# Fused attention and routed FFN on one core: value products issued for two neighbouring key tiles at a time, between the scores of pairs of tiles

## The reference

```python
qkv = layernorm(x) @ Wqkv                 # q: 32 x 16, k: 16, v: 16
scores = einsum('bqhd,bkd->bhqk', q, k) * 16 ** -0.5
scores = where(pos_k <= pos_q, scores + slopes * (pos_k - pos_q), -1e30)
attn = einsum('bhqk,bkd->bqhd', softmax(scores), v).reshape(B, S, H)
x = x + attn @ Wo
y = layernorm(x)
result = y @ W_base.T + b_base
route_w = top-2 of softmax(y @ W_gate.T), renormalised
x = x + result + einsum('bner,eor->bno', (y @ A) * route_w, B)
```

## Time and profile before

| | |
|---|---|
| median of 3 runs | 790.23 us (788.66 to 791.53) |
| profiled execution, first to last instruction | 788.3 us (its own time with what lies around the span is not given apart) |
| TensorE matmul / VectorE / ScalarE / GpSimd busy | 691.0 / 576.1 / 356.9 / 187.6 us |
| granted TensorE clock, mean | 0.956; 1.00 from 170 to 660 us |
| chain that ended last | TensorE 67%, DMA 14%, VectorE 11% |

### The profile page before, as it was taken

The page is one execution under the profiler, slowest core; times in us unless marked ns, Lnnn a source line. Parts: engine busy times, 40 slices in busy tenths (PEclk is TensorE's granted clock), DMA queues, the critical chain, the costliest instruction groups (busy, mean ns, idle before and its releaser), DMA issues.

```text
span 788.3 us, 16078 instructions
## 1 busy us (share of the span) xinstructions
PE 691.0 (88%) x4224; PEld 299.5 (38%) x4224; DVE 576.1 (73%) x1851; ACT 356.9 (45%) x493; POOL 187.6 (24%) x340
## 2 busy tenths in 40 slices
PE   4486535989999999999999999999999996699997
PEld 2243212333344344344334334334433453355553
DVE  6175344989988988989898998898892372366664
ACT  2133010246676666676666666666666410011111
POOL 0010101132242242133233224224233311222221
PEclk9888677999999999999999999999999999699999
DMA  9559799111043052062061085500000189400001
GB/s 235 71 150 128 113 129 224 67 37 64 31 59 55 29 70 43 27 74 52 16 96 39 16 108 91 84 30 16 15 29 30 37 141 162 117 27 27 27 27 53
DMA packets 37592, 56.06 MB, mean 71 GB/s; under 512 B 6028, under 2 KB 19468, under 8 KB 37524
## 3 DMA queue, kind: packets, MB, share of 16 engines
q1 hardware_dynamic: 35468, 49.17, 35.1%
q0 software_dynamic: 1792, 6.29, 2.4%
q10 hardware_dynamic: 288, 0.07, 0.0%
HBM read 35.72 MB, written 19.79 MB: 70 GB/s over the span
## 4 chain that ended last, share of the span: by engine, by line
PE 67%; DMA 14%; DVE 11%; issue 4%; SPq 3%; ACT 1%; DVEq 0%; POOL 0%; POOLq 0%; ACTq 0%
PE psum L606 19%; PE psum L561 16%; PE psum L588 9%; PE psum L630 5%; PE psum L652 5%; DMA q_dram<-work 4%; PE psum L585 4%; DMA arena<-q_dram 4%; DMA x_sb<-in_x 4%; DVE psum L967 3%; PE psum L522 3%; DMA out<-wqkv_sb 3%; DVE negm L972 2%; PE psum L647 1%; PE psum L662 1%
## 5 line engine op out<-in xcount | busy, mean ns | idle before, releaser
L791 ACT ACTIVATE work<-psum 128x1024 f32<-128x1024 f32 (+1 forms) x320 | 289.7, 943 | 161.6 <-PE psum L588 136.2
L967 DVE CUSTOM_DVE_ANT_0 psum<-psum,future 128x384 f32<-128x384 f32 (+3 forms) x512 | 240.0, 517 | 33.1 <-PE psum L561 26.2
L561 PE MATMUL psum<-k_op,arena 106*128 106x512 bf16 (+3 forms) x768 | 209.5, 331 | 35.6 <-DMA arena<-q_dram 20.2
L972 DVE TENSOR_REDUCE negm<-psum 128x1 f32<-128x512 f32 x256 | 163.1, 684 | 29.1 <-PE psum L561 28.4
L606 PE MATMUL psum<-work,v_op 128*32 128x512 f32 (+3 forms) x1536 | 164.3, 500 | 0.4 <-POOL work L1152 0.4
L588 PE MATMUL psum<-arena,k_op 109*128 (+4 forms) x640 | 158.6, 316 | 1.0 <-ACT work L791 0.8
L1152 POOL TENSOR_SCALAR_AFFINE_SELECT work<-work 128x512 f32<-128x512 f32 x128 | 81.6, 637 | 276.5 <-ACT work L791 276.5
L561 PEld LDWEIGHTS psum<-k_op,arena 106*128 (+1 forms) x768 | 69.9, 97 | 192.7 <-issue 95.7
L522 PE MATMUL psum<-work,wqkv_sb 128*128 128x512 f32 (+1 forms) x160 | 83.1, 642 | 15.9 <-issue 15.2
L585 PE MATMUL psum<-arena,k_op 116*128 (+1 forms) x512 | 85.1, 221 | 0.0
L588 PEld LDWEIGHTS psum<-arena,k_op 109*128 109x128 bf16 x640 | 60.3, 98 | 35.7 <-ACT work L791 8.9
(11 more groups left out here) (84 smaller groups left out, 453.1 us busy)
## 6 DMA issues: line engine op xcount, KB each, us to landing
o_dram<-o_sb SPq DMA_DIRECT2D x32, 256.0 KB
q_dram<-work POOLq DMA_DIRECT2D x16, 384.0 KB, 3.1
arena<-q_dram SPq DMA_DIRECT2D x12, 512.0 KB, 17.8
arena<-q_dram SPq DMA_DIRECT2D x48, 128.0 KB, 5.9
arena<-o_dram SPq DMA_DIRECT2D x32, 128.0 KB, 8.9
arena<-rcp_dram SPq DMA_DIRECT2D x32, 128.0 KB, 9.4
out<-wqkv_sb SPq DMA_DIRECT2D x16, 256.0 KB, 2.0
x_sb<-in_x SPq DMA_DIRECT2D x3, 1024.0 KB, 9.0
```

What stands on the lines that cost most here:

```text
L561: last = nc.tensor.matmul(bank[:, a * width:(a + 1) * width], q_op[0:ROW_MAX, bass.ds(col, P)], k_op[0:ROW_MAX, b, k0:k0 + width], start=T ...
L791: nc.scalar.activation(probs[:, n % 4, heads * hp:heads * (hp + 1), 0:w], src, ACT.Exp).then_inc(exp_done, 1)
L967: last = nc.vector.tensor_tensor_reduce(keys, keys, future[:, CH - width:CH], -1.0, 3e38, ALU.add, ALU.min, negm[:, late, 0, j * QT + t:j ...
L972: nc.vector.tensor_reduce(dst, psum[:, idx % NSB, 0:len(js) * width].rearrange("p (a k) -> p a k", a=len(js)), AX_X, ALU.max, negate=True) ...
```

## The change

Only `pe_order` changes. The scores of a tile (both halves) are put in the list without values between them. After every odd tile the values of two tiles are put, those of tile n - 3 and of tile n - 2. The slots are spread over the new list by the same rule.

```diff
     for n, (late, t, off) in enumerate(TILES):
         w = CH - off
         if 1 <= k <= NK:
-            work.append((UH // HALVES[n] * w, ("scores", k - 1, (n, 0))))
-        m, v = (k - 1, n - LAG) if n >= LAG else (k - 2, n - LAG + NTI)
-        if 0 <= m < NK:
-            work.append((UH * (CH - TILES[v][2]), ("values", m, v)))
-        if 1 <= k <= NK and HALVES[n] == 2:
-            work.append((UH // 2 * w, ("scores", k - 1, (n, 1))))
+            work += [(UH // HALVES[n] * w, ("scores", k - 1, (n, hp))) for hp in range(HALVES[n])]
+        if n % 2:
+            for v in (n - 1 - LAG, n - LAG):
+                m, v = (k - 1, v) if v >= 0 else (k - 2, v + NTI)
+                if 0 <= m < NK:
+                    work.append((UH * (CH - TILES[v][2]), ("values", m, v)))
         if k == NK + 1 and n == LAG - 1:
             break
```

## The result

The changed kernel takes 834.45 us (median of 4 runs, 833.15 to 837.35), the kernel before 789.85 on the same chip: a ratio of 1.057, 95% interval 1.055 to 1.060. The profiled execution spans 835.2 us against 788.3.

The account below looks back on a forecast made before the run. TensorE's order was taken to set the time. A net 2.66 us a step gave 37.2 us for 14 steps, plus 2.2 and 1.6 for steps 1 and 16: 41.0 on 790.23, so 831.2 us, range 812 to 845.

Parts of the forecast that it names:

- What bounds the kernel: Steps 2 to 15: TensorE's order sets the time, busy 392.8 of 403.1 us; VectorE has a tenth to spare, ScalarE a third.
- Savings at the ends of runs: Runs of values groups on TensorE: 12 become 10 a step, at 0.21 us each, saving 0.42 us a step.
- Waits in the bursts: Scores in four halves wait for ScalarE to free two PSUM pairs: 0.65 + 0.86 + 0.86 + 0.66 + 1.07 = 4.10 us a step.
- The two copies: Output-bank copies in ScalarE's queue, between halves of tiles 1 and 5: waits of 0.66 us at tile 3, 0.77 at tile 6.
- VectorE's waits of 0.87 go: Tail of the step: TensorE's 0.87 us of waits for VectorE vanish, as VectorE clears its backlog after tile 7's later scores.
- rival 2: Slots before values: VectorE's waits stay or grow, 845 us; chance 0.07.
- The sum: Steps 2 to 15: 4.10 - 0.15 - 0.87 - 0.42 = 2.66 us a step, 37.2 us for 14 steps.
- Steps 1 and 16: First and last attention steps: 2.2 us more in step 1 and 1.6 us more in step 16.
- The signs: Profile after: steps of 31 to 32 us, TensorE's share near 0.90, gap before the copy, tile 6's second half 0.8 us late.
- only the ends count (783): All attention steps: 35 runs of values fewer at 0.21 us give 7.4 us faster, 783 us; chance 0.04.
- Hidden copies (815): ScalarE's two output-bank copies cost nothing, no wait at tile 3, giving 815 us; chance 0.08.
- No difference (790): Whole kernel: new waits only take the place of TensorE's present ones, no difference that counts; chance 0.02.

## Why the prediction was right

The forecast was 831.2 us, the result 834.45. Point by point:

- **What bounds the kernel.** Right: the time follows TensorE's order and its waits, and ScalarE's third of idle time covered nothing.
- **Savings at the ends of runs.** Taken at 0.21 us a run; the trace of the changed kernel gives 0.24. The groups of tiles 10 and 11 take 0.79 together (358.60 to 359.39) against 0.57 + 0.36 apart, 0.14 less, and the way in is 0.10 as before. So 0.48 a step and not 0.42.
- **Waits in the bursts, 4.10 us a step.** Measured 3.99 in the step shown. The large tiles agree within 0.01 at tiles 5 and 7. Tile 1 waits 0.24 less than worked out, since the start of this step runs a little slower than the pace (the slots of 128 and 256 columns from 355.37 take 0.56 us to the next scores where the pace gives 0.33), and a wait absorbs that.
- **The two copies.** Right in place and kind; 0.76 + 0.90 measured for 0.66 + 0.77, and 1.25 us a step came back when they were moved.
- **VectorE's waits of 0.87 go.** This term was mis-sized, and the reading under it was incomplete: 0.87 are not "the only large waits" of the kernel before. Later in the same step three slots of 384, 384 and 512 columns hold TensorE for 0.94 us, where the pace and the way into the values give 0.66, so 0.28 more for VectorE:

```profile
329.02 1.01 PE L561 MATMUL psum<-k_op,arena 106*128 106x384 bf16 x3
329.96 1.07 PE L606 MATMUL psum<-work,v_op 128*32 128x512 f32 x8
```

  Of 1.15 us, then, 0.59 stay in the step of the changed kernel: 0.41 at 373.16 to 373.79, some 0.12 at 362.92 to 363.58, and 0.06 at 375.11 to 375.88. 0.56 go, not 0.87, in the direction of rival 2. The microsecond that TensorE loses on tiles 6 and 7 clears VectorE's backlog in part alone; why not all of it was not tried by itself.
- **The sum.** In the step shown 3.99 - 0.15 - 0.56 - 0.48 = 2.80; it takes 31.59 us where the same step of the kernel before takes 28.54, so 3.05 more. The 0.25 between them are small losses that the walk has no term for, 0.18 of them at the slower start (0.23 over the pace, against 0.05 at 338.06 to 338.54). With the same paces taken off every distance from turn to turn in all 14 steps, waits before scores grow by 4.10 (from 0.18 to 4.28) where the prediction had 4.10 - 0.15, those between slots shrink by 0.58 (1.30 to 0.72) where it had 0.87, and the rest, the ends of runs above all, by 0.50 where it had 0.42. That makes the 3.02 of the two stretches; 2.66 was forecast.
- **Steps 1 and 16.** 0.7 for 2.2 and 2.7 for 1.6. Neither is a clean comparison. In step 1 the kernel before ran at the lower clock for a while (0.66 from 165 to 170 us) and the changed one did not (1.00), which flatters the change; what that is worth, where TensorE also waits for VectorE, I have not worked out. In step 16 it is the changed kernel that had the lower clock; that cost about 1.4 us (below), more than the 1.1 by which the step exceeds the forecast.
- **The signs.** The step of 31.72 us, TensorE's busy share of 0.91 (404.21 of 444.05), the gaps before both copies and the late second half of tile 6 came as said. The sign for rival 2, that waits for L967 and L972 still make over 1 us a step, was badly chosen: the view of waits gives 3.7 us a step, but nearly all of it is on weight loads, and it gave 4.0 before. The starts give 0.72.
- **The rivals.** That only the ends count (783) is refuted, most plainly by the run with all six pairs in one piece, at 873. The Trainium skill has, in "TensorEngine Tiling (Array Packing)", Overview, Key Properties, that changing the tiling mode drains TensorE. The 0.24 us of the rows agree with it, without showing that a drain is what takes them; it is a small term here. Hidden copies (815) did not happen: both had a gap of 1.24 us. No difference (790) fell with the first row of waits.

## What to carry to other kernels

An engine at two thirds of its time can still set the pace if its work arrives in bursts longer than the buffers in between: count how many producers' pieces stand side by side, and compare the time to the one that reuses a buffer (here 1.22 us) with the latency of a round through it (1.72). When one engine's order changes, look at every instruction of the others that stands between two events of it (the copy, here): its right place moves along, and that was two fifths of the loss here. Filler work belongs where the main engine would wait anyway.

## What was unexpected of the hardware

In step 16 of the changed kernel the granted clock of TensorE falls in the stretch with the long waits. Stretches of 5 us, columns as in the earlier trace rows:

```profile
650.00:655.00 5.00, 2.85 (x25) 0.80 (x24) 0.00 (x0) 4.40 (x6) 0.00 (x0) 1.00 0.01 3
655.00:660.00 5.00, 4.06 (x18) 0.90 (x22) 1.18 (x5) 3.96 (x6) 0.00 (x0) 0.73 0.13 51
660.00:665.00 5.00, 5.00 (x32) 2.25 (x24) 0.00 (x0) 2.66 (x4) 0.59 (x1) 0.93 0.01 2
```

TensorE was busy 2.85 of 5 us while ScalarE was busy 4.40; then the clock was at the lower of its two levels (1.2 GHz) for a part of the next stretches, and a pair of values groups took 3.30 us there where it takes 1.92 elsewhere:

```profile
657.91 3.30 PE L606 MATMUL psum<-work,v_op 128*32 128x512 f32 x16
...
665.06 1.92 PE L606 MATMUL psum<-work,v_op 128*32 128x512 f32 x16
```

So waits for another engine cost a second time here, about 1.4 us on that pair. It is not the change's work alone, and not every thin stretch does it. The run without slots between the values has such a dip in step 16 too, and two in the steps before, behind waits for VectorE and for ScalarE; the first is this one:

```profile
265.00:270.00 5.00, 4.09 (x43) 2.44 (x42) 4.17 (x19) 3.52 (x6) 1.61 (x4) 1.00 0.03 7
270.00:275.00 5.00, 4.08 (x25) 1.27 (x25) 3.43 (x11) 1.40 (x2) 1.86 (x3) 0.78 0.14 54
```

The kernel before has one in step 1 (0.66 from 165 to 170 us) and none in attention after it. The changed kernel with the copies moved keeps 1.00 through step 16, where TensorE was busy 3.43 us from 630 to 635 us. I had looked for it nowhere, as each single gap is 1.1 us or less.
